# Three groups of probability-value products instead of four, six probability tiles, new engine orders, and earlier weight splits in a one-core Perceiver layer

## What is computed

```python
def _L0_xattn_ref(q, k, v, mask, wq_w, wq_b, wk_w, wk_b, wv_w, wv_b, wo_w, wo_b):
    ...
    scores = jnp.einsum('bhqd,bhkd->bhqk', qh, kh) / jnp.sqrt(jnp.float32(D_K))
    scores = jnp.where(mask, scores, jnp.float32(-1000000000.0))
    attn = jax.nn.softmax(scores, axis=-1)
    out = jnp.einsum('bhqk,bhkd->bhqd', attn, vh)
    ...
x = x + _L0_xattn_ref(_layernorm(x, axis=-1), ctx_1024, ctx_1024, mask_1x1xSxS2_bf1, ...)
x = x + _L0_attn_ref(_layernorm(x, axis=-1), L0_attn_W_span, L0_attn_W_val, L0_attn_W_out)
x = x + _L0_ffn_ref(_layernorm(x, axis=-1), L0_ffn_t_emb, L0_ffn_sw1, ...)
```

## Time and profile before

| what | value |
|---|---|
| time before, median of 3 runs | 1519.89 us (1517.30 to 1522.43) |
| profiled execution, its own time | 1517.93 us |
| its span, first to last instruction | 1516.0 us |
| mean granted TensorE clock | 0.991 |
| PE busy | 1466.6 us, 97% |
| DVE, ACT, POOL busy | 1005.0, 922.6, 449.4 us |

### The profile page before, as it was taken

How to read it: one execution, slowest core, us unless ns; L and a number is a source line. 1 busy time by engine, 2 the same in 40 slices (tenths; PEclk the granted TensorE clock), 3 DMA queues, 4 the chain that set the end, 5 groups by cost and what they waited for, 6 DMA issues and landing times. The chain is left out here.

```text
span 1516.0 us, 56222 instructions
## 1 busy us (share of the span) xinstructions
PE 1466.6 (97%) x23420; PEld 1245.3 (82%) x23420; DVE 1005.0 (66%) x3958; ACT 922.6 (61%) x1827; POOL 449.4 (30%) x564
## 2 busy tenths in 40 slices
PE   7999999999999999999999999999999999799999
PEld 4788888888888888888888888888888885455698
DVE  5766767677666766767676666766766674755436
ACT  4455666666666665666666566665666664589583
POOL 4433333333333333333333333333333300400043
PEclk9999999999999999999999999999999999899999
DMA  5644444444444443444444444443444241100022
GB/s 159 194 121 114 111 113 116 113 114 116 114 116 111 117 115 106 115 114 116 113 116 114 114 116 113 119 112 105 116 112 118 69 127 62 56 1 1 2 56 84
DMA packets 91757, 156.23 MB, mean 103 GB/s; under 512 B 44896, under 2 KB 55904, under 8 KB 91488
## 3 DMA queue, kind: packets, MB, share of 16 engines
q1 hardware_dynamic: 91216, 151.57, 37.1%
q0 software_dynamic: 288, 1.05, 0.2%
HBM read 69.61 MB, written 4.19 MB: 49 GB/s over the span
## 5 line engine op out<-in xcount | busy, mean ns | idle before, releaser
L680 DVE CUSTOM_DVE_ANT_0 junk<-bank,mask_q 128x400 bf16<-128x400 f32 (+1 forms) x1024 | 547.3, 571 | 180.9 <-issue 175.0
L625 ACT ACTIVATE probs<-bank 128x512 f32<-128x512 f32 (+1 forms) x832 | 467.8, 596 | 123.4 <-PE bank L813 114.8
L594 POOL CAST ctx_hi<-ctx_raw 128x400 fp32r<-128x400 f32 x248 | 122.6, 523 | 784.8 <-PE bank L770 784.8
L813 PE MATMUL bank<-qstack,kstack 104*128 104x128 f16 (+1 forms) x3328 | 290.0, 221 | 0.8 <-ACT probs L625 0.5
L770 PE MATMUL bank<-wv_hi,ctx_hi 128*128 128x256 f32 (+1 forms) x832 | 280.4, 337 | 0.0
L790 PE MATMUL bank<-kstack,qstack 96*128 96x400 f16 (+1 forms) x1024 | 266.9, 336 | 3.4 <-DMA qstack<-q_parts 2.1
L669 DVE SCALAR_TENSOR_TENSOR k_lo<-bank,bk,k_hi 128x400 f16<-128x400 f32 (+1 forms) x256 | 162.0, 633 | 162.5 <-ACT k_hi L635 162.4
L645 ACT ACTIVATE v<-bank 128x256 f32<-128x256 f32 (+1 forms) x416 | 159.8, 384 | 179.1 <-PE bank L770 172.4
L813 PEld LDWEIGHTS bank<-qstack,kstack 104*128 104x128 f16 (+1 forms) x3328 | 215.6, 99 | 60.6 <-issue 18.1
L635 ACT ACTIVATE k_hi<-bank,bk 128x400 f16<-128x400 f32 (+1 forms) x256 | 152.4, 595 | 176.9 <-PE bank L760 168.9
L597 POOL TENSOR_TENSOR ctx_lo<-ctx_raw,ctx_hi 128x400 fp32r<-128x400 f32 x248 | 253.6, 1043 | 0.0
(11 more groups left out here) (170 smaller groups left out, 1633.5 us busy)
## 6 DMA issues: line engine op xcount, KB each, us to landing
ctx_raw<-in_ctxT SPq DMA_DIRECT2D x32, 1602.0 KB, 6.9
kstack<-k_hi SPq DMA_DIRECT2D x512, 100.1 KB, 2.2
kstack<-k_lo SPq DMA_DIRECT2D x256, 100.1 KB, 2.2
weight<-in_w SPq DMA_DIRECT2D x18, 256.0 KB, 2.7
x<-in_xT SPq DMA_DIRECT2D x8, 512.0 KB, 7.1
qstack<-q_parts SPq DMA_DIRECT2D x192, 16.0 KB, 5.3
out_yT<-y SPq DMA_DIRECT2D x8, 256.0 KB, 2.8
weight<-in_sw SPq DMA_DIRECT2D x3, 512.0 KB, 7.3
```

What stands on the lines that cost most here:

```text
L594: nc.gpsimd.tensor_copy(c_hi[:, k, s0:s0 + n], raw[:, k, s0:s0 + n]).then_inc(ctx_hi, 1)
L625: nc.scalar.activation(probs[kt % NP][0:m, GROUPS * h:GROUPS * (h + 1), :], st[h][0:m, :], ACT.Exp, scale=DK ** -0.5 / (UP * UP)).then_inc ...
L680: nc.vector.tensor_tensor_reduce(junk[i % SM][:, 0:n], sm[i % SM][:, 0:n], w["mask_q"][:, s0:s0 + n], 1.0, -3.0e38, ALU.add, ALU.max, part ...
L813: mm = nc.tensor.matmul(st[h][0:m, g * PW:(g + 1) * PW], kstack[b.slot][0:KROWS, p, kt * P:kt * P + m], qstack[b.slot][0:KROWS, p, :], sta ...
```

## The change

- `NP` goes from 4 to 6 probability tiles. The space comes from the query halves `q_hi` and `q_lo`, which move from the tiles that live through the loop to the temporaries of the first stage. As other tiles now lie over them, the select rows of `kstack1`, the ones column of `v1` and ACT's first turn wait until the query halves have been stored.
- `SLOTS` is written anew. Its P steps stand as P x5, P x4 (over the edge of two slots) and P x3, the last joined with the L of the next turn; before they stood as x4, x3, x2 and x3 with L. O goes from behind the fourth key chunk to behind the sixth.
- The orders of the first stage change; the squares get two buffers instead of one, and PE makes 18 small matmuls on `mean_w` before the first means.
- The If of PE is turned round: the masked stream comes first, the one that runs stands in Else.
- The orders of the last turn and the tail change in places. SP loads sw1 and sw3 right behind the first chunk of x. POOL splits them as soon as they are there, sw2 when all outputs of the cross attention are done, and the first w1 pieces when all distance units are done; before, all seven waited for the outputs and for the first turned rows.

```diff
-NP = 4
+NP = 6
...
-                need(act, var, c)
-                nc.scalar.activation(sq[:], xc[c % 2][:], ACT.Square).then_inc(sq_done, 1)
+                need(act, var, c - 1)
+                nc.scalar.activation(sq[c % 2][:], xc[c % 2][:], ACT.Square).then_inc(sq_done, 1)
...
             pe.wait_ge(memsets, 3)
+            for _ in range(18):
+                nc.tensor.matmul(proj_bank[1][:, 0:P], mean_w[:], mean_w[:], start=True, stop=True)
...
-    SLOTS = ["L K K S0 S1", "K K O S0 S1 K K", "S0 S1 K K M M M", "S0 S1 V P P P P M V M M M", "V S0 S1 M V",
-             "M M M V S0 M S1 M", "M V H S0 M V M M S1", "V M S0 S1 H M P P P M", "M H M S0 V S1 M", "V S0 M M M S1",
-             "V S0 M M M S1 P", "P M S0 V M M S1 G H", "S0 V S1 T P N P P"]
+    SLOTS = ["L K K S0 S1", "K K S0 S1", "K K S0 S1 O", "K K M M S0 S1 M", "V V S0 V M M M S1 V M M P P P P P M",
+             "M M V S0 M S1 M M V", "S0 V S1 H M", "S0 V M S1 H M", "M V M M S0 M S1 V M", "S0 M S1",
+             "M V M M M V H M S0 M S1 M P P P", "P S0 M H M S1", "V S0 S1 G T P P P N"]
...
-    FIRST_POOL = "z0 X0 X1 X2 X3 a0 L1 L2 S0 S1 L3 S2 S3 o0"
+    FIRST_POOL = "z0 X0 X1 X2 X3 a0 L1 L2 S0 L3 S1 S2 S3 o0"
...
-    FIRST_PE = """m0 m1 R0 p0 v0 v1 m2 K0 p1 K1 v2 B0 K2 K3 p2 K4 K5 M0 M1 M2 m3 M3 M4 M5 K6 p3 M6 M7 M8 K7 M9 M10 M11 v3 M12 M13 M14
...
+    FIRST_PE = """m0 m1 v0 p0 R0 v1 m2 K0 K1 p1 v2 K2 K3 B0 p2 m3 M0 M1 M2 K4 K5 p3 M3 M4 M5 K6 M6 M7 M8 K7 M9 M10 M11 v3 M12 M13 V0
...
             for i in range(2):
                 sp.wait_ge(q_out[i], 2 * 16 * (NCH // 2))
+            sp.dma_start(kstack[1][KSTACK:KROWS, :, :], ins["c_select"].rearrange("r (p s) -> r p s", s=S2P)).then_inc(d["rows_in"][1], 16)
...
+            for i in range(2):
+                pool.wait_ge(q_out[i], 2 * 16 * (NCH // 2))
             ones_of(pool, v[1])
...
+        for i in range(2):
+            act.wait_ge(q_out[i], 2 * 16 * (NCH // 2))
         turns(act, turn)
...
-        with pe.If(rows_all == S):
+        with pe.If(rows_all < S):
+            run(masked=True)
+        with pe.Else():
             run(masked=False)
-        with pe.Else():
-            run(masked=True)
         rest_body(last_products)
...
-            for c in range(2):
-                load(x[:, :, toks(c)], dram_rows("xT")[:, :, toks(c)], x_in[c])
+            load(x[:, :, toks(0)], dram_rows("xT")[:, :, toks(0)], x_in[0])
+            for n in range(2):
+                load_weight(n)
+            load(x[:, :, toks(1)], dram_rows("xT")[:, :, toks(1)], x_in[1])
...
-            pool.wait_ge(out_done, B)
-            pool.wait_ge(s["rows_done"], 1)
             for n, piece in enumerate(pieces):
+                if piece == "sw2":
+
+                    pool.wait_ge(out_done, B)
+                if n == NSHARED:
+
+                    pool.wait_ge(s["dist_done"], UNITS * NCH)
```

More of the change, by code:

```diff
@@ L132, in build @@
                 kstack=[sb("kstack0", [P, PAIRS, S2P], F16)],
-                q_hi=[sb(f"q_hi{i}", [P, NK, CW], F16) for i in range(2)],
-                q_lo=[sb(f"q_lo{i}", [P, NK, CW], F16) for i in range(2)],
                 k_hi=sb("k_hi", [P, NK, S2P], F16), k_lo=sb("k_lo", [P, NK, S2P], F16),
@@ L202, in queries @@
         xc = [sb(f"xc{i}", [P, NK, CW]) for i in range(2)]
-        sq = sb("sq", [P, NK, CW])
+        sq = [sb(f"sq{i}", [P, NK, CW]) for i in range(2)]
         rstd = [sb(f"rstd{i}", [P, CW]) for i in range(2)]
         q = [sb(f"q{i}", [P, NK, CW]) for i in range(2)]
-        q_hi, q_lo = first_in["q_hi"], first_in["q_lo"]
+        q_hi, q_lo = ([sb(f"{n}{i}", [P, NK, CW], F16) for i in range(2)] for n in ("q_hi", "q_lo"))
         raw, c_hi, c_lo = first_in["raw"], first_in["c_hi"], first_in["c_lo"]
@@ L402, in variances @@
                 for k in range(NK):
-                    i = nc.tensor.matmul(stat_bank[c][:, :], mean_w[:], sq[:, k, :], start=k == 0, stop=k == NK - 1)
+                    i = nc.tensor.matmul(stat_bank[c][:, :], mean_w[:], sq[c % 2][:, k, :], start=k == 0, stop=k == NK - 1)
                 i.then_inc(var, 1)
@@ L505, in cross_attention @@
     FIRST_SP = "s0 Q0 D0 s1 D1 D2 D3 c0 s2 D4 D5 D6 D7 s3 e0 c1"
[L506 to L508 removed]
+    FIRST_POOL = "z0 X0 X1 X2 X3 a0 L1 L2 S0 L3 S1 S2 S3 o0"
+    FIRST_ACT = """Q0 w0 I0 Q1 X0 X1 I1 X2 H0 X3 K0 K1 Q2 K2 K3 H1 I2 H2 K4 Q3 K5 K6 K7 I3 V0 V1 V2 V3 V4 H3 V5 V6 V7 V8 V9 V10 V11 V12"""
+    FIRST_DVE = """C0 r0 C1 w0 l0 G0 C2 L0 K0 K1 G1 K2 K3 Z0 G2 C3 M0 K4 M1 M2 K5 M3 M4 M5 M6 M7 M8 K6 M9 M10 K7 M11 M12 M13 M14 M15 G3
         M16 M17 M18 M19 M20 M21 M22 M23 M24 M25 M26 M27 M28 M29 M30 M31 g0 T0"""
[L510 to L511 removed]
+    FIRST_PE = """m0 m1 v0 p0 R0 v1 m2 K0 K1 p1 v2 K2 K3 B0 p2 m3 M0 M1 M2 K4 K5 p3 M3 M4 M5 K6 M6 M7 M8 K7 M9 M10 M11 v3 M12 M13 V0
+        M14 M15 V1 V2 V3 V4 M16 M17 M18 V5 V6 M19 M20 M21 V7 M22 M23 V8 M24 M25 V9 M26 M27 V10 M28 M29 V11 M30 M31 V12 T0"""
     def turns(eng, emit, loop=False):
@@ L895, in tail @@
     CLS = S // E
-    PE_HEAD = """l0 s0 s1 s2 s3 p0 s4 s5 p1 s6 s7 p2 s8 p3 s9 s10 W0 s11 s12 p4 s13 p5 M0 W1 s14 s15 V0 s16 s17 W2 S0 s18 s19 p6 p7
-        p8 s20 s21 p9 s22 s23 T0 s24 p10 s25"""
+    PE_HEAD = """l0 s0 s1 s2 s3 p0 s4 s5 p1 s6 s7 p2 s8 p3 W0 s9 s10 s11 p4 s12 s13 M0 s14 s15 W1 s16 s17 V0 s18 s19 W2 S0 p5 p6 p7
+        s20 p8 s21 s22 p9 s23 T0 s24 p10 s25"""
     PE_BODY = """M1 A0 p11 p12 V1 A0 A0 W3 A0 S1 A0 A0 T1 A0 A0 M2 X0 X0 U0 X0 X0 V2 A1 O0 S2 A1 A1 Z0 T2 A1 A1 M3 A1 m0 A1 A1 V3 v0
@@ L924, in tail @@
     pieces = ["sw1", "sw3", "sw2"]
-    NFIRST = len(pieces)
+    NSHARED = len(pieces)
     pieces += [("w1", i) for i in range(W_SLOTS)]
@@ L1075, in sync @@
                 load(tile[:], ins[name].rearrange("p (e k) -> p e k", k=NK), s["f_in"])
-            for n in range(len(pieces)):
+            for n in range(2, len(pieces)):
                 load_weight(n)
```

13 lines of the change are left out of this document (6 added, 7 removed).

## The result

The changed kernel takes 1534.63 us in the median of its runs (1533.46 to 1540.86), the kernel before, run beside it, 1518.6 (1517.13 to 1522.43). The ratio is 1.011, with a 95% interval of 1.0075 to 1.0145: slower by 1.1%, about 16 us. The forecast was 1519.6 with a range from 1504 to 1528.

A forecast was written before the change was run, and what follows sets the result against it. TensorE, 97% busy, was taken as the bound through its instructions and stream stops; -7.0 + 1.0 + 14 - 3.2 - 0.7 + 0.5 - 6.4 + 1.5 = -0.3 gave 1517.6 us profiled, 1519.6 median, range 1504 to 1528.

The forecast's parts named there:

- part 2: Loop, TensorE's instruction blocks: denser PV groups use up a block before the next arrives, +14 us, bounds +9 and +20.
- the edges around it: Block edges around the loop's group of five: cost put at 3 us, cancelling against the old group of four.
- brings 3 more: New group of four PV steps in slots 10 and 11, where shorter groups never stalled: 3 us more of stops.
- within some 10 instructions of the group's edge: Loop's old groups of four: a stop needs the block's edge this near, met in 10 of 62 cases.
- rival (b): Loop: blocks cost more, the new group of four like the one around the shift; +22 not +14, 1527.6 us, chance 0.17.
- Rival (a): Loop: blocks keep arriving in time and the group of five adds nothing, 1505.6 us, chance 0.25.
- Part 1: Loop: three PV groups a turn instead of four save TensorE 0.22 us a turn, -7.0 us.
- +1.0 of queueing: Loop: score banks and moved join may queue a little behind VectorE in the new order, +1.0 us, bounds 0 and +4.
- Part 3 and 4: Turned If: tail -3.2 us; first stage: shift 2.2 us earlier, jump costs 3.6, DMA wait hides some, -0.7 us.
- Part 5: Last turn and tail, weight splits moved off VectorE's packing: +0.5 for early splits, -6.4 for packing and bias fold, +1.5 later.
- +1.5 that was put for the w1 splits: Tail: the four w1 splits now meet VectorE's two-input work near 1397 us, +1.5 us, bounds 0 and +4.
- Rival (c): Tail: the gain isn't there, sw2 still covers the chain and w1 splits cost VectorE as before; 1528.5 us, chance 0.10.

The follow-up runs named there:

- experiment 1: The changed kernel with the loop order (SLOTS) of the kernel before, all else as changed: 1500.03 us, ratio 0.9899 to the kernel before.
- experiment 2: The changed kernel with its group of five PV steps cut into three and two: 1521.24 us, ratio 1.0039 to the kernel before.
- experiment 3: The changed kernel with 2 warm-up matmuls instead of 18, loop unchanged: one execution of 1524.54 us.
- experiment 6: The changed kernel with PE's If turned back, so the branch is taken at the loop's end: 1534.55 us, ratio 1.0141 to the kernel before.
- experiment 7: The changed kernel with GpSimd's old waits in the last turn, so no weight is split early: 1538.51 us, ratio 1.0151 to the kernel before.
- experiment 8: The kernel before with only the changed last turn and tail (orders, early weight loads, GpSimd's waits): 1510.01 us, ratio 0.9956 to the kernel before.

## Why the prediction was wrong

**The step that failed is the size in part 2**: "31 x 64/256 = 7.75 turns x (3.2 - 1.79 = 1.4) = 10.9", with "the edges around it are those of the old group of four, 3 us, and cancel against it" and "brings 3 more". The mechanism was right: a dense group uses up a block before the next one is there. The term was mis-sized: +14 us measured 38.4 - 9.7 = +28.7. Three things made it small:

- *The time a block takes.* It was read off two rows as 2.8 to 3.3 us. By the count above, from a block's first instruction to that of the next, the ten blocks of before that ended in a stop had taken 2.8 to 5.0 us, 3.6 on average, so a better figure was there to be read. In after they took 3.0 to 5.7 us, 3.8 on average; the row at 394.51 has 3.76. The twelve stops of slot 4 cost 0.4 to 2.4 us, 1.6 each on average, instead of 1.4.
- *The places that are hit.* With a longer block time a block need not be all PV to be used up too soon. The stops of slot 4 lie over 89 neighbouring positions of the turn (instruction 769 to 857), not 64; 31 x 89/256 = 10.8 turns, and 11 were counted there behind the first turn. Before showed this too: "within some 10 instructions of the group's edge" is some 20 positions of 256 a group and would give 5 cases in the 62, not the 10 that the prediction counted, and the ten stops lie over 28 and 43 positions (247 to 274 and 660 to 702). That group's 19.0 us less the 3.5 of the old one are 15.5, where 10.9 was put.
- *The neighbours.* The group around the shift has the same three products and L in both sets of slots and was put at no change. It went from 3 to 5 stops to 8 to 10 in every kernel with the new slots, +6.2 us. The packet records show how. At instructions 215 to 238 of the turn four edges stop in after and pass in experiment 1, in the same turns, though the block ahead of them is used up about as fast. What differs is when the packet with the next block starts:

```
turn, instruction        after: block used, packet starts, stop      old slots: block used, packet starts
18, 215                  3.44    +2.87    2.2                        3.41    -0.50    no stop
6, 219                   3.21    +2.22    1.2                        3.08    -0.66    no stop
25, 234                  2.67    +1.58    1.1                        2.80    -0.85    no stop
13, 238                  2.42    +1.68    1.4                        2.63    -0.96    no stop
```

The start is counted in us from the first instruction of the block in use. In the first three of the four the edge one block earlier, in slots 10 and 11, had itself stopped in after (by 1.0, 1.2 and 0.6 us), and experiments 2, 3 and 6 have such pairs too. Behind a stop the next packet is late in general: in after it never starts earlier than 1.06 us into the new block, where the median behind the 140 edges that pass is 0.94. So the new group of four costs its own 6.9 us, where 3 was put, and some of its stops lead to another one block later. What sets the start of a packet, and what the new order of the last slot adds (S0, S1 and the shift directly ahead of the group, where a value chunk stood between S0 and S1), no run separates.

The forecast's own rival (b), dearer blocks and the new group like the one around the shift, described what happened, at +22; even this was short. Rival (a), blocks that arrive in time, is out: its time of 1505.6 would have needed no stop in the group of five. A busy DMA ring isn't the cause either: the packets took 0.88 to 1.67 us at the 27 stops and the same 0.88 to 1.67 at the edges that passed. Of the loop's 167 blocks in after the 127 that were used in 3.7 us or longer ended without a stop, and 27 of the 40 shorter ones ended in one of 0.3 to 2.4 us.

**Part 1**, -7.0 with +1.0 of queueing: the clean turn fell from 37.30 to 37.15, the shortest from 37.19 to 37.10; cutting the group of five in two brought back 0.2. That is -3 to -6 over 31 turns. Right in kind, a little large.

**Part 3 and 4**, the branch and the first stage: the jump costs 3 to 4 us at either end, as read from the earlier trace rows. At the start it hides the 1.8 to 2.5 us that PE would wait for the DMA, as said. The first shift came 2.8 us earlier (2.2 said). Start and first turn together gave +0.4 us where -0.7 was said; the lower clock behind the jump (1.8 us) and a block stop of 0.8 us in the first turn weren't in the sum. The warm-ups did nothing for the time of the first shift. Their 36 records took 6.81 us from 1.19 on, 0.19 each (0.21 said), and the eight means behind them ran from 7.83 to 11.43, 0.45 us each (0.46 said), where before had 0.84 each from 5.42 to 12.14. That the slow means stand at the lower clock level was a reading: the record of the granted clock begins, at 1.00, only at 11.35 us in before and 6.5 in after. The ratio of 1.8 between the two durations is that of 0.33 to 0.18 us of the key matmuls, where the record has 0.50 and 1.00.

**Part 5**, the splits: with the branch, -7.6 was said of the tail, and it gave -11.0. The prediction left VectorE's normalisation at 3.73 us because sw2 would still cover it. It took 1.29: the first operation of sw2, which starts a microsecond before it, doesn't slow it there (row at 1306.82), and it begins earlier as well. By the end of packing (1315.29, 50.2 us after the last turn's shift; before 1301.00, 62.5 us after it) the tail had gained 12.3 us, and 1.3 were given back later. That is near the +1.5 that was put for the w1 splits, but no run shows that it is theirs. Rival (c), no gain in the tail, is out by experiments 7 and 8.

The sum by measured terms: +27.9 for stops in turns 1 to 30, +1.4 for the clock, -3.1 for one group less (not measured by itself but what is left of those turns' 26.2, and within the 3 to 6 above), +0.4 for start and first turn with its stop of 0.8, -11.0 for the tail: +15.6, the difference of the two spans. The other signs that the prediction named came: the least turn at 37.10 us (37.08 said), no idle PE where PE_HEAD ends, a gap of 4.25 us after the first shift, packing at 2.6 us.

## What to carry to other kernels

Where an engine's instruction stream has dense stretches, count instructions as well as time: on this kernel TensorE stopped at 27 of the 40 blocks of 256 instructions that it used in less than 3.7 us and at none of the others, so 13 PV products of 64 instructions each were better here in groups of at most three or four with slower matmuls between them than in one group of five, though each group fewer saves 0.1 to 0.2 us. Two dense groups about a block apart can hurt each other, as a late block was followed by a late packet here (1.06 us or more into the block in use, in all 27 cases of after). A block's edge drifts through the loop when a turn isn't a whole number of blocks (1387 instructions here, 5 x 256 + 107), so a single clean turn shows nothing; look for turns of the same work and other lengths, and for the remainder of the instruction's number at each pause. To size such a stop, count all of the ones that the trace holds, not two of them. When a change has several parts, try them apart: here turns 1 to 30 lost 26 us and hid a tail worth 9 to 11.

## What was not expected of the hardware

- A stop of TensorE of some 2 us was followed, in 3 of the 27 cases of after, by 3.4 us at a granted clock of 0.50, which cost another 1.4 us by the estimate above. The stretch began 1.6 and 1.2 us behind the stop's end in two of them and 0.2 us before it in the third. The length of the stop doesn't decide it alone: none of the 27 of experiment 6, up to 2.2 us long, was followed by such a stretch, and two of experiment 1, of 1.6 us, were.
- A taken branch of TensorE cost 3 to 4 us (3.18 before, 2.9 and 3.79 in experiments 8 and 6), and 3.5 at the start of the loop in after (4.25 less the 0.73 that experiment 6 has there), where the granted clock was 0.50 for 6.8 us around it.
- At every one of the 27 stops TensorE went on only 1.24 to 1.63 us after the end of the packet with the next block.
- GpSimd's multiply of one input (2.79 us at 1305.78) ran beside VectorE's normalisation of two inputs (1.29 us for two, at 1306.82) without slowing it, while the splits' subtraction beside it made it 3.45 us in experiment 7 (row below). The multiply isn't free everywhere: in experiments 8 and 6 the normalisation started 0.6 and 0.5 us behind it instead of 1.0, and took 1.56 and 1.71 us.

```profile
1307.63 2.84 POOL L1121 TENSOR_TENSOR sw_lo<-weight,sw_hi 128x1024 fp32r<-128x1024 f32 x1
```
